# A transformer layer on one core: three moves in the order of its MLP stage

## The reference

```python
ada = silu(c) @ Wada.T + bada                      # six rows of 512 for each of the 4 samples
shift_msa, scale_msa, gate_msa, shift_mlp, scale_mlp, gate_mlp = split(ada, 6)
h = rmsnorm(x) * (1 + scale_msa) + shift_msa
q, k, v = split(h @ Wqkv.T + bqkv)                 # q and k are normalised per head
o = softmax(q @ k.T) @ v
x = x + gate_msa * (o @ Wproj.T + bproj)
h = rmsnorm(x) * (1 + scale_mlp) + shift_mlp       # y = x is normalised: here stand the inverse roots
h = gelu(h @ Wfc1.T + bfc1) @ Wfc2.T + bfc2
x = x + gate_mlp * h                               # the output
```

## Time and profile before

| | |
|---|---|
| median of 3 runs | 1808.54 us (1808.01 to 1810.1) |
| the profiled execution's own time | 1807.75 us |
| its span in the trace | 1805.9 us |
| PE busy in the span | 1727.0 us, 96% |
| DVE, ACT, POOL busy in the span | 59%, 51%, 21% |
| PE busy from 1060 to 1806 us (the MLP stage) | 730.13 of 746.00 us |
| granted TensorE clock, mean of the span | 0.991 |
| store of a result tile, issue to landing | 2.0 us |

### The profile page before, as it was taken

The page is one execution under the profiler, slowest core; times in us unless marked ns, Lnnn a source line. Parts: engine busy times, 40 slices in busy tenths (PEclk is TensorE's granted clock), DMA queues, the critical chain, the costliest instruction groups (busy, mean ns, idle before and its releaser), DMA issues.

```text
span 1805.9 us, 23336 instructions
## 1 busy us (share of the span) xinstructions
PE 1727.0 (96%) x8424; PEld 1154.2 (64%) x8424; DVE 1073.1 (59%) x1319; ACT 919.7 (51%) x1136; POOL 374.9 (21%) x305
## 2 busy tenths in 40 slices
PE   5999999999999999999999999999999999999998
PEld 3655555555555555555334787878788887878786
DVE  6578788888898988878777545142322324142301
ACT  3476676777777777778886432222222212221221
POOL 3100111011000110000140233333332323333332
PEclk8999999999999999999999899999999999999999
DMA  7645454555555555465765202010020202010000
GB/s 262 148 102 163 120 138 126 149 143 142 139 131 147 147 136 135 129 155 138 179 159 203 67 18 65 18 53 23 15 66 6 64 17 64 17 52 23 17 18 24
DMA packets 122242, 176.92 MB, mean 98 GB/s; under 512 B 29568, under 2 KB 43904, under 8 KB 121136
## 3 DMA queue, kind: packets, MB, share of 16 engines
q1 hardware_dynamic: 118064, 160.60, 33.3%
q10 hardware_dynamic: 3296, 12.62, 1.9%
q0 software_dynamic: 800, 2.62, 0.5%
HBM read 124.87 MB, written 50.92 MB: 97 GB/s over the span
## 4 chain that ended last, share of the span: by engine, by line
PE 44%; issue 29%; DVE 11%; POOL 9%; ACT 5%; DMA 2%; SPq 1%; POOLq 0%; ACTq 0%; DVEq 0%
PE scores L525 9%; PE pv L542 8%; PE gemm L606 7%; PE scores L1319 5%; POOL act_parts L1251 5%; DVE sums L807 4%; ACT probs L724 4%; PE gemm L619 4%; PE pv L1336 3%; PE gemm L1336 2%; PE aux L572 2%; POOL y L1249 2%; PE aux L559 1%; DVE raw L832 1%; DVE raw L878 1%
## 5 line engine op out<-in xcount | busy, mean ns | idle before, releaser
L724 ACT ACTIVATE probs<-scores,shift 128x1024 f32<-128x1024 f32 x512 | 548.9, 1114 | 194.5 <-PE scores L525 177.9
L807 DVE TENSOR_TENSOR sums<-sums,probs 128x2048 f32<-128x2048 f32 x186 | 439.5, 2363 | 31.2 <-ACT probs L724 26.8
L525 PE MATMUL scores<-q_stack,k_stack 128*128 128x512 f32 x1024 | 358.0, 435 | 6.6 <-ACT probs L724 6.4
L1319 PE MATMUL scores<-w_hi,act_parts 128*128 128x512 f32 x1024 | 317.5, 391 | 0.0
L525 PEld LDWEIGHTS scores<-q_stack,k_stack 128*128 128x128 f32 x1024 | 173.4, 189 | 200.3 <-issue 105.2
L1251 POOL TENSOR_TENSOR act_parts<-act_full,act_parts 128x512 fp32r<-128x512 f32 x128 | 172.5, 1348 | 513.0 <-ACT act_parts L1182 512.4
L542 PE MATMUL pv<-probs,v 128*32 128x512 f32 x2048 | 250.7, 598 | 0.4 <-ACT probs L724 0.4
L1319 PEld LDWEIGHTS scores<-w_hi,act_parts 128*128 128x128 f32 x1024 | 190.7, 188 | 38.6
L1319 PE MATMUL scores<-w_lo,act_parts 128*128 128x512 f32 x512 | 199.4, 389 | 0.0
L1389 DVE TENSOR_TENSOR y_next<-pv,p_bias 128x512 f32<-128x512 f32 x28 | 19.3, 691 | 297.9 <-PE pv L1291 297.9
L1182 ACT ACTIVATE act_parts<-act_full 128x512 fp32r<-128x512 f32 x128 | 80.9, 632 | 223.2 <-PE scores L1319 222.2
(11 more groups left out here) (169 smaller groups left out, 1949.7 us busy)
## 6 DMA issues: line engine op xcount, KB each, us to landing
k_stack<-parts_scratch SPq DMA_DIRECT2D x128, 256.0 KB, 5.0
q_stack<-parts_scratch SPq DMA_DIRECT2D x128, 256.0 KB, 5.1
parts_scratch<-parts SPq DMA_DIRECT2D x62, 512.0 KB, 3.0
inverse<-inverse_scratch SPq DMA_DIRECT2D x128, 64.0 KB, 2.1
heads_out<-o_out SPq DMA_DIRECT2D x32, 256.0 KB, 5.2
out<-result SPq DMA_DIRECT2D x32, 256.0 KB, 2.0
heads<-heads_out SPq DMA_DIRECT2D x28, 256.0 KB, 3.9
x_tile<-in_x SPq DMA_DIRECT2D x28, 256.0 KB, 2.8
```

The costliest lines, as they stand in the source:

```text
L525: mm = nc.tensor.matmul(scores[p][:, i, :], k_stack[s][:, h, j * P:(j + 1) * P], q_stack[half][:, h, :], start=True, stop=True)
L724: nc.scalar.activation(probs[L % RING][:, 2 * p:2 * p + 2, :], scores[p][:], ACT.Exp, bias=small["shift"][:]).then_inc(exp_done, 1)
L807: nc.vector.tensor_tensor(sums[:], a[:], probs[l % RING][:], ALU.add).then_inc(added, 1)
L1319: mm = nc.tensor.matmul(acc[t], act_parts[m % 2][:, b, t * P:(t + 1) * P], w2[a][:, m, :], start=(m == 0 and i == 0), stop=(m == NM - 1 an ...
```

## The change

Three moves, and two small helpers for the third.

1. On POOL the inverse roots of the next block are issued in `prepare` at step 12 instead of step 13, so ahead of the low part of step 13 instead of behind it. DVE's clamp stays at step 13.
2. On PE, in blocks 0 to 6, turn 2 goes ahead of the last token tile (a quarter) of down 13, instead of behind it.
3. In block 7 lift 15 goes ahead of down 12, and downs 14 and 15 are made tile by tile: tile 0 of step 14, tile 0 of step 15, tile 1 of step 14, and so on. Step 15's high and low part go to a buffer of their own (`heads_parts`, which no projection uses any more), and tiles 2 and 3 are closed in `y_norm` instead of `result`, without the wait for a store.

```diff
+    def final(c):
+        return isinstance(c, int) and c == NC - 1
+    def parts_of(c, m):
+        return heads_parts[:].rearrange("p s k n -> p s (k n)") if final(c) and m == NM - 1 else act_parts[m % 2]
+    def result_of(c, t):
+        return y_norm[t % 2] if final(c) and t >= CT // 2 else result[t % 2]
...
-            if m >= 2:
+            if final(c) and m == NM - 1:
+                act.wait_ge(proj_mm, CT * NC)
+            elif m >= 2:
                 act.wait_ge(down_mm, (NM - 1) * c + m - 1)
...
         def prepare(c, m):
-            if m == NORM:
+            if m == NORM - 1:
                 pool.wait_ge(y_clamped, norms_before(c) + 1)
                 nc.gpsimd.tensor_tensor(y_inv[:], y_sqc[:], small["minus_half"][:, 0:CT], ALU.pow).then_inc(y_inverse, 1)
...
                 lift(c, m)
                 if more and m == NM - 2:
                     turn_tile(c + 1, 0)
+                if not more and m == NM - 2:
+                    lift(c, NM - 1)
                 if m >= LAG:
                     down(c, m - LAG, first_two + last_two)
...
             if more:
                 turn_tile(c + 1, 1)
-            lift(c, NM - 1)
-
-            down(c, NM - 3, first_two + last_two)
-            if more:
+                lift(c, NM - 1)
+                down(c, NM - 3, (0, 1, 2))
                 turn_tile(c + 1, 2)
-            down(c, NM - 2, first_two)
-            if more:
+                down(c, NM - 3, (3,))
+                down(c, NM - 2, first_two)
                 turn_tile(c + 1, 3)
-            down(c, NM - 2, last_two)
-            down(c, NM - 1, first_two + last_two)
+                down(c, NM - 2, last_two)
+                down(c, NM - 1, first_two + last_two)
+            else:
+                down(c, NM - 3, first_two + last_two)
+                for t in range(CT):
+                    down(c, NM - 2, (t,))
+                    down(c, NM - 1, (t,))
...
-            r = result[t % 2]
+            r = result_of(c, t)
             dve.wait_ge(acc_mm, n + 1)
-            dve.wait_ge(out_stored[t % 2], 16 * (CT // 2 * c + t // 2))
+            if not (final(c) and t >= CT // 2):
+                dve.wait_ge(out_stored[t % 2], 16 * (CT // 2 * c + t // 2))
```

More of the change, by code:

```diff
@@ L1074, in finish @@
             sp.dma_start(dram["out"].rearrange("b (h n) d -> (b h) n d", h=NH)[c, t * P:(t + 1) * P, :],
-                         result[t % 2][:]).then_inc(out_stored[t % 2], 16)
+                         result_of(c, t)[:]).then_inc(out_stored[t % 2], 16)
         return step, last
@@ L1181, in mlp @@
                 act.wait_ge(acc_mm, CT * c)
-            nc.scalar.activation(act_parts[m % 2][:, 0, :], act_full[m % 2][:], ACT.Copy).then_inc(act_hi, 1)
+            nc.scalar.activation(parts_of(c, m)[:, 0, :], act_full[m % 2][:], ACT.Copy).then_inc(act_hi, 1)
         return step, last
@@ L1250, in mlp @@
             pool.wait_ge(act_hi, NM * c + m + 1)
-            nc.gpsimd.tensor_tensor(act_parts[m % 2][:, 1, :], act_full[m % 2][:], full(act_parts[m % 2][:, 0, :]), ALU.subtract).then_inc(act_lo, 1)
+            nc.gpsimd.tensor_tensor(parts_of(c, m)[:, 1, :], act_full[m % 2][:], full(parts_of(c, m)[:, 0, :]), ALU.subtract).then_inc(act_lo, 1)
         return step, last
@@ L1318, in down @@
                 for i, (a, b) in enumerate(pairs):
-                    mm = nc.tensor.matmul(acc[t], act_parts[m % 2][:, b, t * P:(t + 1) * P], w2[a][:, m, :],
+                    mm = nc.tensor.matmul(acc[t], parts_of(c, m)[:, b, t * P:(t + 1) * P], w2[a][:, m, :],
                                           start=(m == 0 and i == 0), stop=(m == NM - 1 and i == 2))
```

## The result

| | before | after |
|---|---|---|
| median of 6 runs | 1808.39 us (1807.89 to 1810.1) | 1798.6 us (1796.66 to 1801.16) |
| ratio, 95% interval | | 0.9939 (0.9928 to 0.9949) |
| profiled execution, its span | 1807.75, 1805.9 us | 1798.42, 1796.6 us |

A second measurement of the same two kernels gave 0.9938 (0.9925 to 0.9952). The change makes the kernel faster by 0.6%, 9 to 13 us. The forecast was 1796.8 us, 0.9935 of the median it started from.

The account below looks back on a forecast made before the run. PE was taken to bound the MLP stage. Blocks 1 to 6 give 9.0 us, block 0 0.2 and the end 2.5, 11.7 in all: 1796.8 us from a median of 1808.54, range 1794.5 to 1799.6.

Parts of the forecast that it names:

- The roots, blocks 1 to 6: Block ends: roots issued earlier end PE's wait at turn 0, 1.10 us a block plus 0.06 for the slower restart.
- Turn 2: Block ends, blocks 0 to 6: turn 2 ahead of down 13's last quarter removes turn 3's wait, 0.34 us each.
- the covers of 1.0 and 0.5 us: Time to spare ahead of down 15 (1.0) and the next block's first lift (0.5), so no new wait there.
- Block 0: Square freed from POOL, normalise then caught by the low part: turn 0 loses 0.11, turn 3 gains 0.34, 0.2 us in all.
- The end: Block 7 tile by tile: DVE's last instruction ends 2.49 us earlier, with ends of 2.8 and 1.5.
- PE's delay: Block 7, down 15 of tile 0: PE waits for step 15's low part, 0.35 us, ends nothing and 1.3.
- A: Rival: block 0 gains as well and PE does not wait at the end, 13.1 us gained, 1795.4 us; chance 0.25.
- B: Rival: turn 0 waits for something else, 1.10 us stays lost in six blocks, 1803.4 us; chance 0.04.
- C: Rival: covers run short by up to 0.4 us a block, the end gives 1.5 only, 1800.6 us; chance 0.08.
- D: Rival: TensorE's clock falls 2% when PE has no gaps, costing 14 us, so slower at 1810.8 us; chance 0.03.
- signs of being wrong: About 1 us still waited at turn 0, a new wait at down 15 or a first lift, or a stage clock below 1.00.

Follow-up runs that it names:

- roots_loop: Changed kernel, but block 0's inverse roots stay at step 13; only blocks 1 to 6 have them at step 12: 1797.73 us, ratio 0.9936.
- after_again: The changed kernel once more without an edit, with a new profile: 1797.88 us.
- y_first: Changed kernel, but in block 0 at step 13 DVE makes y and the clamp before the low part of w2's last rows: 1793.28 us, ratio 0.9917.
- hold_low: Changed kernel, but in block 0 POOL holds step 13's low part until DVE has normalised the first two tiles: 1795.76 us, ratio 0.9924.
- low_on_dve: As `y_first`, and in block 7 DVE instead of POOL makes step 15's low part: 1792.92 us, ratio 0.9902.
- before_again: The kernel before the change once more without an edit, with a new profile: 1809.37 us.
- after: The changed kernel's first measurement and profile, against the kernel before: 1798.6 us, ratio 0.9939.
- roots_only: The kernel before with only move 1, inverse roots at step 12: 1802.58 us, ratio 0.9965.

## Why the prediction was right

**What bounds it.** Right: with PE's idle spots gone, loop blocks shrank by just those, from 101.38 us to 99.85, and PE is busy for all of it.

**The roots, blocks 1 to 6.** Right: 1.16 us a block forecast, 101.34 - 100.16 = 1.18 measured by itself.

**Turn 2.** Right: 0.34 forecast, 0.35 measured by itself, and the covers of 1.0 and 0.5 us stood. Together 18.25 us for the block end, 18.28 forecast. Block 1's missing 0.25 us is a wait of its first projection (its row of twelve matmuls lasts 3.01 us instead of 2.88) for a tile of attention's output that landed later: VectorE could take it up 4.7 us after its load was issued, against 4.1 in `roots_loop`. It is there in `after_again` too (0.18), and absent in `y_first`, `hold_low` and `roots_loop`; why the load was slower is not known.

**Block 0.** The mechanism was right, with both its halves: the square freed, the normalise caught. A loss of 0.11 us was forecast for turn 0, a gain of 0.04 came (5.12 to 5.08 us after lift 14). The low part began 0.07 us ahead of the normalise, where the prediction took 0.05. What it left out is the low clock behind the wait, 1.6 us: it took the earlier trace rows, where nothing slow stands behind 2.24 us of waiting, as the rule, and had no term and no rival for it.

The Trainium skill (SBUF — State Buffer, "Who interferes with whom") says that issue order and not the shape of the operation decides who blocks. The trace agrees: the same normalise pair took 1.93 us behind the low part, 1.00 ahead of it in `hold_low`. That settles what the prediction left open, whether this normalise contends at all.

**The end.** Right: 2.5 us forecast, 2.50 in the profiles, 2.4 by itself. PE's delay was 0.34, forecast 0.35, and its reason, two low parts in one queue, is shown by `low_on_dve`.

**The sum.** The gain was sized right; the two profiled executions by themselves hide it. They differ by 9.3 us and not 11.7, and the missing 2.4 are the 1.60 of the low clock, which the first profile of the kernel before was spared, 0.65 of a later start of the MLP stage, 0.25 of block 1's wait and under 0.1 of other small differences, less the 0.16 by which block 0 did better than forecast apart from the clock. The two later profiles, `before_again` and `after_again`, both have the low clock. Between them block 0's end is 0.43 us shorter (22.65 to 22.22), blocks 1 to 6 8.72 (608.01 to 599.29), block 7 to DVE's last instruction 2.54 (91.50 to 88.96), and the rest 0.03: 11.7 us from lift 14 of block 0 on, which is the forecast. The medians gave 9.8 us the first time and 11.3 the second.

The absolute time was 1.8 us above the forecast, inside the range. The range allowed for scatter and for a short cover, not for a low clock, so that it held the time in spite of the missed clock is partly luck. The forecast started from a median of three runs, 1808.54 us; later medians of the same kernel were 1808.39 to 1810.08. How many of those three runs had the low clock is not known, so it can't be said how much of the 1.8 us is the clock. Block 1's wait is 0.25 of it, and scatter ahead of block 0 can be as large as all the rest, in the attention stage, which the change does not touch: lift 14 of block 0 starts between 1081.95 and 1085.43 us in the twelve profiles, whose programs are the same up to shortly before it. The granted clock differs there as well (from 200 to 400 us 0.99 in the first profile of the kernel before, 0.97 in `before_again`), but what sets the scatter stays open.

**The rivals.** A failed by its first half (block 0 gave nothing) and by PE's wait at the end. B and C did not come: no wait stayed, no cover ran short. D did not come: the loop's blocks are busy from end to end at 1.00. But one of the prediction's own signs of being wrong did, a clock below 1.00 in the stage: 0.83 from 1088 to 1098 us. The clock mattered from the other side than in D: it fell behind a wait, not where PE had no gaps, and it fell in the kernel before as well.

The Trainium skill (TensorE: Matmul & The Clock Gate, "Part 1") has activity open the gate. The traces agree in direction: 1.00 from 1080 to 1100 us in the three profiles without the wait, 0.91 in seven of the eight with the wait of 2.2 us.

## What to carry to other kernels

Where one engine is the bound and works in a written order, walk back each of its few idle spots to the queue place that causes it: an instruction that waits only behind its neighbour is worth the whole gap, and here the gain, added up from start times, came out within 0.1 us a block. The wait of 2.2 us on TensorE mostly cost another 1.6 us behind it, so look at the granted clock behind it in more than one profile. And an in-order queue that is moved ahead of a wait also moves what is behind it, on to whatever the other engine does next.

## What the runs showed of the hardware

- Behind a wait of 2.20 to 2.25 us the granted clock was at the lower level for a time in seven of eight profiles, and from turn 0 to turn 1 PE took 4.83 or 4.84 us in these seven instead of 3.24, 1.6 more. Behind a wait of 1.27 us it stayed at 1.00, in the one profile there is.
- GpSimd and VectorE hold each other up, and the one that began first goes ahead. Beside a GpSimd subtraction that had begun first, a square of 0.69 us took 1.67, a normalise of 0.55 took 1.42 and a pair of 1.00 took 1.93; they ended 0.55, 0.29 and 0.74 us after the subtraction did, so nearly all of their work came behind it. The other way round, the subtraction at 1083.81 took 1.65 us instead of 1.29; it had begun 0.19 us behind this VectorE addition:

```profile
1083.62 0.69 DVE L1397 TENSOR_TENSOR y_next<-y_next,x_tile 128x512 f32<-128x512 f32 x1
```

- A GpSimd instruction queued behind the inverse roots started 0.06 to 0.07 us before VectorE's normalise, which waited for the roots' semaphore, in the three profiles where the two raced (`after`, `after_again`, `roots_only`). The queue won each time.
